# A graph-attention kernel: each step waits for its own chunk, landings counted in order by SyncE, and the broadcasts are issued from ScalarE's queue

## The reference

```python
x   : (3125, 128) normal;  src : (50000,) uniform in 0..3124
dst = sorted((3125 * uniform(50000) ** 2.0).astype(int32))

def _transformer_conv(x, src, dst, qw, qb, kw, kb, vw, vb, sw, sb):
    q, k, v = ((x @ w + b).reshape(N, 2, 128) for w, b in ((qw, qb), (kw, kb), (vw, vb)))
    alpha = jnp.einsum('ehd,ehd->eh', q[dst], k[src]) / sqrt(128)
    m     = segment_max(alpha, dst)
    ex    = jnp.exp(alpha - m[dst])
    w     = ex / (segment_sum(ex, dst)[dst] + 1e-16)
    agg   = segment_sum(w[:, :, None] * v[src], dst)
    return agg.mean(axis=1) + x @ sw + sb

h   = conv(x; layer 1) + x @ lin1_w + lin1_b
out = conv(h; layer 2) + h @ lin2_w + lin2_b
return layernorm(x + out)
```

## Time and profile before

| what | value |
|---|---|
| median of 3 runs | 1222.47 us (1220.92 to 1222.86) |
| time of the profiled execution | 1220.84 us |
| its span from first to last instruction | 1219.0 us |
| granted TensorE clock, mean | 0.939 |
| PE busy | 1002.1 us, 82% |
| DVE busy | 984.2 us, 81% |
| ACT busy | 785.4 us, 64% |
| POOL busy | 756.6 us, 62% |
| DMA, mean | 71 GB/s |

### The profile page before, as it was taken

One profiled execution on the slowest core, in us unless ns is written; L12 is line 12 of the kernel. 1 busy time (PEld: TensorE's weight loads), 2 busy tenths in 40 slices (PEclk: granted clock), 3 DMA queues, 4 the chain that ended last, 5 costly groups with the idle time before them and its releaser, 6 DMA issues.

```text
span 1219.0 us, 32111 instructions
## 1 busy us (share of the span) xinstructions
PE 1002.1 (82%) x6792; PEld 778.5 (64%) x6792; DVE 984.2 (81%) x5260; ACT 785.4 (64%) x2594; POOL 756.6 (62%) x804
## 2 busy tenths in 40 slices
PE   4778888888797889888986787879788978898887
PEld 3546667767575667677753565657576757676775
DVE  5798989888787888899487777777877878888976
ACT  1356767777575769676274364758575758678755
POOL 7777777777777777300077777777777777771000
PEclk9988999999999989999897799999998989999988
DMA  5323333333322333100133332323332323230001
GB/s 141 88 76 89 89 80 89 82 86 79 80 79 80 79 80 81 45 2 1 53 103 79 80 80 70 87 73 85 78 81 72 86 73 88 71 88 26 2 2 53
DMA packets 51941, 87.04 MB, mean 71 GB/s; under 512 B 16699, under 2 KB 25169, under 8 KB 51761
## 3 DMA queue, kind: packets, MB, share of 16 engines
q0 software_dynamic: 25024, 51.30, 16.7%
q1 hardware_dynamic: 24145, 32.62, 9.2%
q10 hardware_dynamic: 2592, 1.07, 0.4%
HBM read 81.58 MB, written 3.34 MB: 70 GB/s over the span
## 4 chain that ended last, share of the span: by engine, by line
PE 27%; POOL 18%; issue 18%; DVE 17%; DMA 13%; ACT 4%; DVEq 2%; SPq 0%; POOLq 0%; ACTq 0%
POOL gathered L424 18%; PE ps L703 14%; DMA gathered<-h_rows,src_e 8%; PE ps L691 7%; DVE junk L980 5%; DVE acc L1011 5%; DMA gathered<-in_x,src_e 5%; ACT whot L525 4%; PE ps L802 2%; PE ps L797 1%; PE ps L786 1%; DVE apart L991 1%; DVE max_b L1049 1%; DVEq L285 1%; DVEq L1011 1%
## 5 line engine op out<-in xcount | busy, mean ns | idle before, releaser
L703 PE MATMUL ps<-gathered,whot 128*128 x3328 | 573.3, 300 | 86.6 <-ACT whot L525 64.4
L525 ACT ACTIVATE whot<-apart,below 128x128 f32<-128x128 bf16 x1664 | 551.5, 388 | 124.3 <-DVE apart L991 108.8
L703 PEld LDWEIGHTS ps<-gathered,whot 128*128 128x128 f32 x3328 | 457.5, 200 | 167.3 <-issue 128.5
L980 DVE SCALAR_TENSOR_TENSOR junk<-ps,gathered 128x129 f32<-128x129 f32 x1664 | 413.3, 286 | 149.0 <-issue 76.4
L691 PE MATMUL ps<-table,hot_t 128*128 x2496 | 443.4, 287 | 62.9 <-DVE junk L980 40.9
L424 POOL DMA_INDIRECT gathered<-in_x,src_e x391 | 377.1, 965 | 119.7 <-issue 75.6
L424 POOL DMA_INDIRECT gathered<-h_rows,src_e x391 | 374.7, 958 | 118.9 <-issue 74.4
L1011 DVE TENSOR_TENSOR acc<-ps,acc 128x258 f32 x832 | 350.7, 421 | 19.3 <-PE ps L703 9.8
L691 PEld LDWEIGHTS ps<-table,hot_t 128*128 128x128 bf16 x2496 | 251.0, 101 | 154.6 <-issue 110.0
L509 ACT ACTIVATE apart<-col_b,ndl_e 128x128 bf16<-128x128 bf16 x618 | 239.2, 387 | 0.0
L980 DVE DVE_READ_ACCUMULATOR junk<-ps,gathered 128x1 f32 x1664 | 135.8, 82 | 0.3
(11 more groups left out here) (176 smaller groups left out, 554.0 us busy)
## 6 DMA issues: line engine op xcount, KB each, us to landing
dl_bc<-local_dst_rows SPq DMA_DIRECT2D x104, 256.0 KB
gathered<-in_x,src_e POOLq DMA_INDIRECT x391
gathered<-h_rows,src_e POOLq DMA_INDIRECT x391
h_rows<-table SPq DMA_DIRECT2D x6, 256.0 KB, 2.3
out<-x_rows SPq DMA_DIRECT2D x6, 256.0 KB
table<-in_L_gnn_q_w ACTq DMA_DIRECT2D x2, 128.0 KB
table<-in_L_gnn_k_w ACTq DMA_DIRECT2D x2, 128.0 KB
wv<-in_L_gnn_v_w ACTq DMA_DIRECT2D x2, 128.0 KB
```

What stands on the lines that cost most here:

```text
L525: last = nc.scalar.activation(whot[:, c % UN, h, :], apart[:, c % UN, :], ACT.Exp, scale=FAR, bias=below[:, j % 2, h, o:o + 1])
L703: last = nc.tensor.matmul(bank_u[n % NB][:, h * C1:(h + 1) * C1], whot[:, c % UN, h, :], gathered[:, bass.ds(slot, 1), :].rearrange("p o c ...
L980: last = V.scalar_tensor_tensor(out=junk[:, t % 2, h, :], in0=bank_t[n % NB][:, h * C1:(h + 1) * C1], scalar=1.0, in1=gathered[:, bass.ds( ...
```

## The change

SyncE counts the landings of the chunks, in order: it waits for the eight `got` semaphores in turn and adds one to `landed[layer]` for each. `tiles_of` takes the place of `bins_of` on PE and loads two values a step from the new tile `tile_i`: the tile b, and the number of chunks up to the step's own, min(t - b, 390) + 1. `step_t` on PE waits until `landed[layer]` has reached that number; `step_alpha` on DVE no longer waits for a landing, and `newest` is gone. The broadcasts from the third on are issued from ACT's queue, in slots 0, 8, 16 and so on (`spread_ahead`), the first two by SyncE before it begins to count. The stores of the row sets 1 and 2 come after the eighth chunk (`EARLY_CHUNKS`). Two operations on DVE make `tile_i` in the preparation.

```diff
--- before.py
+++ after.py
@@ -53,6 +53,7 @@
 SKIP_SLOT, SKIP_EVERY = 5, 3
 T_AHEAD = 2
 LATE_ROWS, LATE_DST, LATE_MASKS = 1, 6, 7
+EARLY_CHUNKS = 8
 NGR = -(-BINS // G)
 C1 = F + 1
 CW = HEADS * C1
@@ -173,6 +174,7 @@
         ring_f = sb("ring_f", [P, 3, CT])
         ndl_e = sb("ndl_e", [P, STEPS])
         bin_i = sb("bin_i", [1, STEPS], i32)
+        tile_i = sb("tile_i", [1, STEPS, 2], mybir.dt.uint16)
         slot_i = sb("slot_i", [1, STEPS], i32)
         link = sb("link", [2, STEPS + 1])
         linkneg = sb("linkneg", [2, STEPS + 1])
@@ -248,6 +250,7 @@
         h_saved = [sem(f"h_saved{k}") for k in range(2)]
         rows_out = [sem(f"rows_out{k}") for k in range(ROW_SETS)]
         dl_in = [sem(f"dl_in{k}") for k in range(2)]
+        landed = [sem(f"landed{l}") for l in range(2)]
 
         banks = [bank_s, bank_r]
         block = ctx.enter_context(nc.Block())
@@ -280,16 +283,20 @@
                 skip_runtime_bounds_check_because="a step's bin is step - chunk, within 0..24 by the staircase")
             return v
 
+        def tiles_of(etype, step):
+            _, v = nc.values_load_multi_w_load_instructions(
+                tile_i[0:1, step:step + RB, :].rearrange("o s v -> o (s v)"), engines=[etype], min_val=0, max_val=CHUNKS,
+                skip_runtime_bounds_check_because="a step's tile of nodes, within 0..24 by the staircase, and the number of "
+                                                  "chunks up to its own, 1..CHUNKS")
+            return [(v[2 * k].with_bounds(min_val=0, max_val=BINS - 1), v[2 * k + 1].with_bounds(min_val=1, max_val=CHUNKS)) for k in range(RB)]
         def slots_of(etype, step):
 
             _, v = nc.values_load_multi_w_load_instructions(
                 slot_i[0:1, step:step + RB], engines=[etype], min_val=0, max_val=RING - 1,
                 skip_runtime_bounds_check_because="a chunk's slot is its number modulo RING")
             return v
-
-        def newest(t):
-
-            return min(t, CHUNKS - 1)
 
         def slots():
 
@@ -318,6 +325,16 @@
         def made(l, c, dve):
 
             return l * by_dve.count(dve) + by_dve[:c + 1].count(dve)
+        dl_flat = dl_d.rearrange("(o s) e -> o (s e)", o=1)
+        per_layer = STEPS // BC
+        def spread_rows(eng, n):
+            q = n % per_layer
+            eng.dma_start(dl_bc[:, n % 2, :], dl_flat[:, q * BC * P:(q + 1) * BC * P].to_broadcast([P, BC * P])
+                          ).then_inc(dl_in[n % 2], 16)
 
 
         @block.sync
@@ -349,22 +366,17 @@
                 for j in range(G * w, min(G * (w + 1), NBLK)):
                     sp.dma_start(dl_d[STARTS[j]:STARTS[j + 1], :], dl_rb[0:SIZES[j], j, :]).then_inc(rows_out[w], 16)
             store_rows(0)
-            dl_flat = dl_d.rearrange("(o s) e -> o (s e)", o=1)
-            per_layer = STEPS // BC
+            sp.wait_ge(rows_out[0], 16 * G)
+            for n in range(2):
+                spread_rows(sp, n)
             for l in range(2):
-                for q in range(per_layer):
-                    n = l * per_layer + q
-                    if l == 0 and q == 2:
+                for c in range(CHUNKS):
+                    n = l * CHUNKS + c
+                    if l == 0 and c == EARLY_CHUNKS:
                         for w in range(1, ROW_SETS):
                             store_rows(w)
-                    if n >= 2:
-                        sp.wait_ge(S["hot_t_ready"], n - 1)
-                    w = BLOCK_OF[(q + 1) * BC - 1] // G
-                    if l == 0 and (q == 0 or w != BLOCK_OF[q * BC - 1] // G):
-                        sp.wait_ge(rows_out[w], 16 * len(range(G * w, min(G * (w + 1), NBLK))))
-                    sp.dma_start(dl_bc[:, n % 2, :],
-                                 dl_flat[:, q * BC * P:(q + 1) * BC * P].to_broadcast([P, BC * P])
-                                 ).then_inc(dl_in[n % 2], 16)
+                    sp.wait_ge(got[n % GQ], 16 * (n // GQ + 1))
+                    sp.sem_inc(landed[l], 1)
                 if l == 0:
 
                     for g in range(NGR):
@@ -502,6 +514,17 @@
                     nc.scalar.copy(below[:, j % 2, :, 0:r], bank_s[:, 256:256 + 2 * r].rearrange("p (h e) -> p h e", h=HEADS)
                                    ).then_inc(S["below_ready"], 1)
 
+            def spread_ahead(l, a):
+                n = l * per_layer + a // BC + 2
+                if n < 2 * per_layer:
+                    act.wait_ge(S["hot_t_ready"], n - 1)
+                    if l == 0 and n < per_layer:
+                        w = BLOCK_OF[(n + 1) * BC - 1] // G
+                        if w != BLOCK_OF[n * BC - 1] // G:
+                            act.wait_ge(rows_out[w], 16 * len(range(G * w, min(G * (w + 1), NBLK))))
+                    spread_rows(act, n)
             def far_apart(l, c):
 
                 if l * STEPS + c >= UN:
@@ -536,6 +559,8 @@
                                 row_set(w)
                     if a is not None and a + T_AHEAD + 1 <= BINS:
                         split(l, a + T_AHEAD + 1)
+                    if a is not None and a % BC == 0:
+                        spread_ahead(l, a)
                     k = None if a is None else a - LATE_MASKS - 2
                     if k is not None and 0 <= k < BINS:
                         if l == 0 and k == 0:
@@ -680,13 +705,14 @@
                                             wskip[:, l, :], start=True, stop=True)
                 last.then_inc(S["skip_mm"], 1)
 
-            def step_t(l, t, b):
+            def step_t(l, t, b, count):
 
                 n = l * STEPS + t
                 if t % BC == 0:
                     pe.wait_ge(S["hot_t_ready"], n // BC + 1)
                 if n >= NB:
                     pe.wait_ge(S["alpha_ready"], n - NB + 1)
+                pe.wait_ge(landed[l], count)
                 for part in range(3):
                     last = nc.tensor.matmul(bank_t[n % NB][:, 0:CW], hot_t[:, n // BC % 2, t % BC, :],
                                             table[:, bass.ds(b, 1), part, :].rearrange("p o c -> p (o c)"),
@@ -748,14 +774,14 @@
 
                         for k in range(a + PE_AHEAD if a else 0, min(a + PE_AHEAD + 1, STEPS)):
                             if k == 0:
-                                b = bins_of(PE, 0)
+                                b = tiles_of(PE, 0)
                             elif k % RB == 0:
                                 b = b_next
                             if k % RB == RB - LOAD_AHEAD and k + LOAD_AHEAD < STEPS:
-                                b_next = bins_of(PE, k + LOAD_AHEAD)
+                                b_next = tiles_of(PE, k + LOAD_AHEAD)
                             if k < BINS:
                                 pe.wait_ge(S["part3"], l * BINS + k + 1)
-                            step_t(l, k, b[k % RB])
+                            step_t(l, k, *b[k % RB])
                     if s is not None:
                         scan(l, *s)
                     for c in cs:
@@ -877,6 +903,8 @@
             V.tensor_copy(bq_wide, bq[:, 0, 0:1].to_broadcast([P, P])).then_inc(S["bq_ready"], 1)
             dve.wait_ge(S["prep_mm"], 2)
             V.tensor_tensor(bin_i[:, :], step_f[0:1], bank_r[64:65, 0:STEPS], ALU.subtract)
+            V.tensor_tensor(tile_i[:, :, 0], step_f[0:1], bank_r[64:65, 0:STEPS], ALU.subtract)
+            V.tensor_scalar(tile_i[:, :, 1], bank_r[64:65, 0:STEPS], float(CHUNKS - 1), 1.0, ALU.min, ALU.add)
             V.tensor_copy(slot_i[:, :], bank_r[96:97, 0:STEPS])
             V.tensor_tensor(firsts, bank_r[0:2, 0:STEPS], step128[0:2], ALU.subtract)
             copied(1, V.tensor_tensor(lasts, bank_r[32:34, 0:STEPS], step128[0:2], ALU.subtract))
@@ -970,11 +998,8 @@
 
             def step_alpha(l, t, slot):
                 n, j = l * STEPS + t, BLOCK_OF[t]
-                m = l * CHUNKS + newest(t)
                 if n >= 2:
                     dve.wait_ge(S["alpha_ready"], n - 1)
-                if t == newest(t):
-                    dve.wait_ge(got[m % GQ], 16 * (m // GQ + 1))
                 dve.wait_ge(S["t_ready"], n + 1)
                 for h in range(HEADS):
                     last = V.scalar_tensor_tensor(
```

## The result

The changed kernel takes 1532.7 us (median of 4 runs, 1529.1 to 1534.0), the kernel before 1221.7 us beside it: the ratio is 1.2542 (95% interval 1.2515 to 1.2569). The forecast was 1186 us, the range 1171 to 1212. It is 347 us off, and on the other side.

The account below looks back on a forecast made before the run. Steps were taken to be bound by lockstep with POOL's gathers through a too-late landing wait. Gains of 37.8 and 2.8 us, 40.6, less costs of 3 and 1.2 gave 36.4 us: 1222.5 to 1186 us, range 1171 to 1212.

Parts of the forecast that it names:

- What bounds the kernel: Steps run in lockstep with POOL's gathers, 1.26 us each against a possible 1.11, as alpha waits for chunk t, not t - b.
- Rival A: DVE's "issue" idle time isn't landings, so only labelled waits go: 21.4 us less 4.2 of costs, 1205 us; chance 0.11.
- Limit 1: DVE's removable idle time ahead of alpha that ends with a landing: 26.0 + 4.6 us in layer 0, 46.4 + 4.6 in layer 1.
- limit 2: How far a step can move before meeting its own chunk: near step 340, 16 gathers less 1.3 us, 18.9 us a layer.
- rival B: The cap near step 340 never binds; each layer gains the lead at step 391, 25.2 us: 1172 us; chance 0.05.
- Cost (a): PE's added wait for landed before each of 832 step_t: 0 to 42 us, taken as 3.
- Cost (b): tiles_of on PE loads 16 values in place of 8: 0, since issued four steps, over 4 us, before need.
- Cost (c): Two more DVE operations in the preparation, each like one of 583 ns: 1.2 us, bounds 0 and 1.2.
- Cost (d): 102 broadcasts issued from ACT's queue, at most 0.45 us each, 46 us in all, within ACT's free time: 0.
- Cost (e): SyncE counts 782 landings, a wait and an increment each, off every engine: 0 to 2 us, taken as 0.
- Rival C: PE's sequencer becomes the bound if the wait needs three instructions a step, 0.153 us: 49 us slower, 1235; chance 0.08.
- The relay's hops: Two more semaphore hops through SyncE, 0.25 us each, within 1.3 us of longer way from landing to alpha, bounds 0.8 and 1.4.

Follow-up runs that it names:

- own_const_dve: Kernel before, but step_alpha on DVE waits for the step's own chunk, t - b, written as constants of this input: 1173.1 us against 1223.0, ratio 0.9605.
- act_bcast: Kernel before, with only the broadcasts from the third on issued from ACT's queue: 1221.7 us against 1223.9, ratio 0.9989.
- count_by_reg: Whole change, but PE loads 8 int32 tiles as before and works out the count in a register: 1240.4 us against 1223.9, ratio 1.0145.
- own_const_pe: Whole change, but the count PE waits for is a constant of this input and tiles load as before: 1179.1 us, ratio 0.9637 to the kernel before.
- count_on_dve: Whole change, but step_alpha on DVE waits for the count, from one 16-int32 load: ratios 1.0069 and 1.0122, only where the kernel before takes 1635 to 1648 us.
- ahead7_uint16: Changed kernel, with PE's load issued seven steps ahead in place of four: 1816 and 1830 us, where the kernel before takes 1635 and 1647.

## Why the prediction was wrong

**What bounds the kernel: right.** The lockstep of steps and gathers, the lead of b chunks, and "issue" as landing time are borne out by own_const_dve: counted over the whole span, the waits of alpha by "issue" and by a landing fall from 102.2 to 57.5 us, and the time by 49. Rival A, with 21.4 us, is refuted by the 45 to 51 us.

**Limit 1 and limit 2: right in mechanism, small.** The sum was 40.6 us with 2 * 1.3 us for the longer way, 43 without it; measured are 45 to 51. Layer 0 gave 21.7 us by the start of layer 1's gathers, against 18.9 and a share of the 2.8; layer 1 gave the other 27 us. The formula took the cap near step 340 for exact and left only 2.8 us for everything behind it, but the stretch from the last gather of a layer to its end became 25.0 and 26.7 us shorter. That is what rival B has: the lead at the end of a layer, 21 * 1.26 = 26.5 us without the longer way. (Its time of 1172 leaves out the 4.2 us of costs; with them it is 1176.) The landing waits were to shrink to a third: they did so in the middle of layer 0, from 26.0 to 6.9 us, but in that of layer 1 they fell by 17 us only, from 46.4 to 29.3. How the rest of layer 1's gain comes about isn't shown.

**Cost (a), the wait on PE: right as far as the noise tells.** 3 us, the longer way 2.6 us, 5.6 together; measured 6, by the ratios 4 (0 to 8).

**Cost (b), the load: the step that failed.** It said of `tiles_of` that 16 values in place of 8 cost 0, since the load is "issued four steps, over 4 us, before its values are needed; 0, and if two loads are needed for it 104 * 0.59 would still run under that cover". Two errors stand in it. The duration was carried over from a load of another type: it is 3.79 us, not 0.59 or 1.18. And the cover isn't there: a load is no transfer in the background, it holds the sequencer, and only what is already queued runs on beside it. With the cover that was assumed, even 3.79 us would have fitted under "over 4 us"; without it, the load alone makes 270 of the 311 us. No row of the kernel before showed a load of uint16 values, and yet this cost got no range.

**Cost (c)** wasn't measured by itself. **Cost (d): right.** An issue on ACT takes 0.326 us, not 0.453, and act_bcast shows no effect. **Cost (e)** right as far as it was looked at: a wait and increment of SyncE, L379, takes 17 ns, and behind none of the 104 loads did PE wait for the count.

**Rival C: right mechanism, wrong owner.** It put PE's sequencer as the way to a slower kernel and its price in instructions of 51 ns. The sequencer did become the bound, through the load, at 104 * 3.2 / 832 = 0.40 us a step, nine times its point of balance of 0.044. As stated, with its instructions in each step, it is count_by_reg; it was given 8 in 100.

**The relay's hops.** No row tells the time of a hop by itself; own_const_pe is 4 to 6 us behind own_const_dve with all of the longer way in it. The figure of 50 to 100 ns for reading a semaphore in the Trainium skill (Advanced Engine Details and Errata, section Miscellaneous Facts) isn't contradicted, but no run here shows a read by itself: L715, a wait, takes 51 ns and own_const_pe leaves room for two reads. The 0.7 us that the prediction worked out from it is below what the runs can tell.

## What to carry to other kernels

A value read from memory into a sequencer's register was time of PE here, however early the load was issued; price such a load by values and by type. Whether it is cheaper on another engine is open, as count_on_dve has no run where before takes 1222 us. When a step is made to wait for less, first measure the freed lead by itself, with constants, and only then pay for the general form: here the lead was worth 50 us, constants on PE kept 44 and a loaded int32 count 32, while a computed count made the kernel 17 us slower than before and a loaded uint16 count 311. Where a wait that is named as the releaser comes exactly once in n steps, look for what else happens once in n steps.

## What the runs showed of the hardware

- On PE's sequencer a load of registers takes 1.92 us for 8 uint16 values and 3.79 for 16, 0.234 us for each further value; for int32 it takes 0.59 us for 8 and 1.105 for 16, 0.064 for each further value.
- Nothing behind the load on PE's sequencer is issued until it ends, at all 104 loads of the changed kernel and of ahead7_uint16_b.
- With 103 stalls of 3.1 us on average, PE's mean granted clock fell from 0.939 to 0.808, and the time at 1.2 GHz rose from 148 to 589 us; the clock fell in 86 of the 104 loads or up to 1.5 us behind.
- A register operation on PE's sequencer takes 32 to 44 ns, a move 29, a wait 51. A move and two operations a step, in place of a wait, turned a gain of 44 us into a loss of 17.
